# Moving the adding transfers of a weight row ahead of the sums of squares, and a store of zeros ahead of a load

## The chip, the cores and the metric

The kernel runs on one core of one Trainium2 chip. The metric is the device time of one execution in microseconds (us). The kernel before takes 734.59 us (median of three runs, 734.38 to 735.34).

## The reference, cut to what matters

Two blocks work on 4096 tokens (16 sequences of 256) of width 256. The first is a gated recurrence, the second a mixture of 16 experts, of which each token uses four.

```
x = x + layernorm(L0_attn(layernorm(x)))     # xp = x @ W_in.T, gates = xp @ W_gate.T + b_gate,
                                             # a scan over the sequence, then @ W_out.T
h = layernorm(x)
logits = h @ router_weight.T + router_bias   # top 4 of 16, softmax over the four
gate_up = einsum('th,ehd->etd', h, gate_up_proj) + gate_up_proj_bias
glu = min(gate, 7) * sigmoid(1.702 * min(gate, 7))
out = einsum('etd,edh->eth', (clip(up, -7, 7) + 1) * glu, down_proj) + down_proj_bias
x = x + layernorm(sum over experts of router_score * out)
```

A normalised row sums to zero over its 256 columns. The kernel uses that: it leaves the last column of the normalised row out, puts a one in its place, subtracts the last row of each expert's gate_up weights from all its other rows, and puts the bias where the last row was. The diff touches this subtraction.

## The kernel before, in words

**Stages.** The tokens go through the recurrence in eight blocks of 512, in a software pipeline of steps `step(s)`: block s gets its gates, block s-1 its scan and output product, block s-2 its second normalisation and its router logits, block s-3 its expert rows. Then come 143 tiles of 128 rows, each of one expert, and at the end the sums are normalised and stored. Each engine runs its own list of instructions in the order in which it is written, and waits on semaphores in front of an instruction; what stands behind a waiting instruction waits too. Within a step the lists go by gate chunk c = 0 to 7, and a place in them is written here as (s, c). Tables give the weight work its places: `SQUARE_AT` for `squares(n)`, `CONV_DN` and `CONV_GU` for `high(n)`.

**Weights.** W holds 24 parts of 1024 columns in float32: 8 of the down weights and 16 of the gate_up weights, one for each expert. `squares` on ScalarE (ACT) takes the sum of squares of a part, all 24 one after the other; from these comes the scale with which `high` and `low` (on VectorE, DVE) turn the parts into two float16 halves. The down parts are squared at (0, 6) to (1, 3). The gate_up parts c0, c1 and c2 have the place (1, 5), c3 (1, 6), c4 and c5 (1, 7), c6 (2, 0), c7 (2, 2), and c15, the last, (3, 6).

**The negative row.** SyncE (SP) loads the last rows (`nrow`), DVE turns their sign, SP stores them to `neg_mem`; then GpSimd (POOL) issues 16 adding transfers, one for each expert, of 512 KB each: the row from `neg_mem`, spread over 128 partitions, is added to the part in W by the DMA engines. In the kernel before such a transfer waits until both parts of its pair have been squared. SP writes the bias row into W's last partition when all 16 have landed (`bias_in`), and the first `high` of a gate_up part, at (4, 2), waits for that.

**SP's queue.** SP issues all plain transfers in the order of its list. `ring_x(b)` stores block b-5 of the residual (`store_x1`, when `r3_ready` says that it is normalised), waits for the store to land, and loads block b of x into the same buffer. Behind `ring_x(5)` stand two transfers of 4 MB each that fill the two DRAM buffers `sums` with zeros; the tile stage adds into these. `stats_x(5)` on DVE, at the start of step 3, needs block 5.

Of the kernel before, what the change touches and what calls it, by code (L numbers as in the profile page):

```python
# [19 lines left out]
P = 128  # L20
BATCH, SEQ, DIM = 16, 256, 256
TOKENS = BATCH * SEQ
# [6 lines left out]
NTILE = TOKENS // P  # L29
GATES = 4 * DIM  # L30
CHUNKS = GATES // P
E, TOPK, FF = 16, 4, 256
# [28 lines left out]
SUMS = 2  # L61
BATCHES = ((0, 1, 2, 3), (4, 5, 6), (7,))
PART = 1024
PARTS_GU, PARTS_DN = E * KT * 2 * FF // PART, E * KT * DIM // PART
PARTS = PARTS_GU + PARTS_DN
# [67 lines left out]
def build(nc, x, w_in, w_gate, b_gate, rms_w, w_out, w_router, b_router, w_gu, b_gu, w_dn, b_dn,  # L133
# [3 lines left out]
    ALU = mybir.AluOpType  # L137
# [5 lines left out]
    with ctx:  # L143
        def sb(name, shape, dt=f32):
            return ctx.enter_context(nc.sbuf_tensor(name, shape, dt))

        def sem(name):
            return ctx.enter_context(nc.semaphore(name))
# [6 lines left out]
        sums = [nc.dram_tensor(f"sums{a}", [TOKENS + (E + SPARE) * P, DIM], f32, kind="Internal").ap() for a in range(SUMS)]  # L155
# [15 lines left out]
        zero = sb("zero", [P, DIM])  # L171
# [117 lines left out]
        s_moe = [sem(f"s_moe{n}") for n in range(PARTS_GU // 2)]  # L289
        squared, peak_ready, peak_mm = sem("squared"), sem("peak_ready"), sem("peak_mm")  # L290
        scale_ready, high_done, low_done = sem("scale_ready"), sem("high_done"), sem("low_done")
        blk_in = [sem(f"blk_in{b}") for b in range(NBLK)]
        nrow_in, nrow_ready, nrow_out, minus_done = sem("nrow_in"), sem("nrow_ready"), sem("nrow_out"), sem("minus_done")
        bias_in, bias_out, brow_ready = sem("bias_in"), sem("bias_out"), sem("brow_ready")
        s_down, wr_ready = sem("s_down"), sem("wr_ready")
        hi_ready, lo_ready, one_ready = sem("hi_ready"), sem("lo_ready"), sem("one_ready")
# [26 lines left out]
        zero_ready, zero_sent, x1_sent = sem("zero_ready"), sem("zero_sent"), sem("x1_sent")  # L323
# [17 lines left out]
        def order(n):  # L341

            return PARTS_GU + n if n < PARTS_DN else n - PARTS_DN
# [4 lines left out]
        def held(table, top, eng, first, n):  # L348

            _, values = nc.values_load_multi_w_load_instructions(  # L350
                table[0:1, ds(first, n)], engines=[eng], min_val=0, max_val=top,
                skip_runtime_bounds_check_because="the table holds counts, capped at the last spare tile")
            return values
# [35 lines left out]
        def source(c):  # L389
            return W[:, (place(c) + 1) * PART:(place(c) + 2) * PART]  # L390
# [13 lines left out]
        def _(sp):  # L404
# [30 lines left out]
            sp.dma_start(bias_mem, brow).then_inc(bias_out, 16)  # L435
            sp.wait_ge(nrow_ready, 1)
            sp.dma_start(neg_mem, nrow).then_inc(nrow_out, 16)

            def store_x1(t):
                sp.wait_ge(r3_ready, t + 1)  # L440
                sp.dma_start(out_v[:, BT * t:BT * (t + 1), :], block_x(t)).then_inc(x1_sent, 16)

            def ring_x(b):
                store_x1(b - XRING)
                sp.wait_ge(x1_sent, 16 * (b - XRING + 1))
                sp.wait_ge(x2_ready, b - XRING + 1)
                load_x(b)

            ring_x(XRING)
            sp.wait_ge(zero_ready, 1)  # L450
            for a in range(SUMS):
                sp.dma_start(sums[a][0:TOKENS, :].rearrange("(n p) d -> p n d", p=P),
                             zero[:, :].unsqueeze(1).to_broadcast([P, NTILE, DIM])).then_inc(zero_sent, 16)
            ring_x(XRING + 1)
            sp.wait_ge(minus_done, 16 * E)
            sp.wait_ge(bias_out, 16)
            sp.dma_start(W[P - 1:P, (GU0 + 1) * PART:(GU0 + 1 + PARTS_GU) * PART]
                         .rearrange("o (e k x) -> o e k x", e=E, k=KT)[:, :, KT - 1, :],
# [323 lines left out]
        def _(act):  # L782
# [86 lines left out]
            def squares(n):  # L869
                c = order(n)  # L870
                if c == PARTS_GU:
                    act.wait_ge(s_down, 16 * PARTS_DN // 2)
                if c < PARTS_GU and c % 2 == 0:
                    act.wait_ge(s_moe[c // 2], 16)
                act.wait_ge(squared, n + 1)
                nc.scalar.activation(junk, source(c), ACT.Square, accum_out=ssq[:, c:c + 1]).then_inc(squared, 1)  # L876

# [13 lines left out]
            def weight_work(s, c):  # L891
                for n, at in enumerate(SQUARE_AT):
                    if at == (s, c):
                        squares(n)
                for n, at in enumerate(CONV_DN + CONV_GU):
                    if at == (s, c):
                        high(n)
# [130 lines left out]
        @block.gpsimd  # L1028
        def _(pool):
            def wait(s, n):  # L1030
                pool.wait_ge(s, n)
                if not isinstance(n, int):
                    pool.nop(nofuse=True)

            def scatter(t):

                b = t % 2
                per = BT * TOPK // 2
                pool.wait_ge(slot_ready, t + 1)
                pool.wait_ge(lo_ready, t + 1)  # L1040
                for jk in range(BT * TOPK if t < NBLK - 2 else AHEAD):
                    lane = jk % 2
                    if t or jk >= 2:
                        pool.wait_ge(rows_sent[lane], 16 * (per * t + jk // 2))
                    idx = slot[b][:, jk:jk + 1].bitcast(u32)
                    pool.indirect_dma_start(routed, bass.IndirectOffsetOnAxis(ap=idx, axis=0),  # L1046
                                            rows[b][:, jk // TOPK, :], None).then_inc(rows_sent[lane], 16)

            pool.wait_ge(nrow_out, 16)
            for e in range(E):  # L1050
                if e % 2 == 0:
                    pool.wait_ge(s_moe[e // 2], 16)
                    pool.wait_ge(squared, 2 + PARTS_DN + e + 1)
                pool.dma_start(W[:, (GU0 + 1 + e) * PART:(GU0 + 2 + e) * PART].rearrange("p (k x) -> p k x", k=KT),  # L1054
                               neg_mem[e:e + 1, :].unsqueeze(1).to_broadcast([P, KT, 2 * FF]),
                               accum_op=ALU.add).then_inc(minus_done, 16)

            for t in range(NBLK - 1):
                scatter(t)

            def late_row(n):
                t, jk = divmod(BT * TOPK * (NBLK - 2) + AHEAD + n, BT * TOPK)
                if jk == 0:
                    pool.wait_ge(slot_ready, t + 1)
                    pool.wait_ge(lo_ready, t + 1)
                idx = slot[t % 2][:, jk:jk + 1].bitcast(u32)
                pool.indirect_dma_start(routed, bass.IndirectOffsetOnAxis(ap=idx, axis=0),
                                        rows[t % 2][:, jk // TOPK, :], None).then_inc(rows_sent[jk % 2], 16)

            for j in range(TILES):  # L1070
                u = j % YU
                pool.wait_ge(meta_in[j % MU], 16 * (j // MU + 1))
                if j == 0:
                    pool.wait_ge(zero_sent, 16 * SUMS)
                pool.wait_ge(y2_ready, j + 3)
                if j >= SUMS:
                    pool.wait_ge(y_sent[(j - SUMS) % YU], 16 * ((j - SUMS) // YU + 1))
                pool.indirect_dma_start(sums[j % SUMS], bass.IndirectOffsetOnAxis(ap=dst[j % MU], axis=0),  # L1078
                                        yb[u], None, compute_op=ALU.add).then_inc(y_sent[u], 16)
                if j % 2 and j // 2 < 2 * BT * TOPK - AHEAD:  # L1080
                    late_row(j // 2)

            pool.wait_ge(x1_sent, 16 * (NBLK - 1))
            for g in range(NBLK - 1):
                pool.wait_ge(yz_ready, g + 1)
                pool.dma_start(out_v[:, BT * g:BT * (g + 1), :], z[g], accum_op=ALU.add).then_inc(out_sent, 16)
# [480 lines left out]
```

## Time and profile before

| what | value |
|---|---|
| median of three runs | 734.59 us |
| the profiled execution's own time | 735.17 us |
| its span | 733.4 us |
| TensorE (PE) busy | 626.0 us, 85% |
| DVE busy | 516.5 us, 70% |
| ACT busy | 459.2 us, 63% |
| POOL busy | 395.2 us, 54% |

Times in the trace are counted from the span's start. The steps of the recurrence take up its first 260 us or so. The page's share of DMA is the mean over the core's 16 DMA engines of the time that their packets took; as packets overlap, it can be somewhat over one. SPq is SP as it issues transfers; the duration of such a row is the time that the issue took.

### The profile page before, as it was taken

What the parts mean: (1) busy time and instruction counts of PE and PEld (TensorE: products, weight loads), DVE (VectorE), ACT (ScalarE), POOL (GpSimd) and SP (SyncE); (2) the same over time, 40 slices, a digit from 0 to 9 for tenths busy, and PEclk for the clock granted to TensorE, in tenths of its full rate; (3) what the DMA queues carried; (4) which work ended last, traced back from release to release, by engine and by line L of the source; (5) the groups of instructions that cost most, each with busy time, mean ns of one, the idle gap of its engine ahead of it and who ended that gap; (6) DMA issues with size and microseconds to landing.
All of it is one profiled execution on the core that took longest, in us unless ns stands there. A gap on an engine that the chain in (4) does not pass through costs nothing.

```text
span 733.4 us, 13293 instructions
## 1 busy us (share of the span) xinstructions
PE 626.0 (85%) x3690; PEld 400.4 (55%) x3690; DVE 516.5 (70%) x1472; ACT 459.2 (63%) x929; POOL 395.2 (54%) x298
## 2 busy tenths in 40 slices
PE   6988979797999848799989999999999999984640
PEld 2454636373655546466656666666666666653420
DVE  3726596968878897877877777777777777650794
ACT  3788887647575643576656776766767767661044
POOL 0004212346777676667788776666666656576022
PEclk9999999679989956999999999999999999996555
DMA  7979999773232335456678977777776766755998
GB/s 243 419 308 150 219 266 300 184 198 118 88 120 89 118 118 154 130 103 115 118 133 174 186 154 117 109 116 115 109 115 103 116 111 104 107 65 59 317 226 145
DMA packets 110695, 114.34 MB, mean 156 GB/s; under 512 B 31426, under 2 KB 100306, under 8 KB 108962
## 3 DMA queue, kind: packets, MB, share of 16 engines
q0 software_dynamic: 34784, 49.70, 40.0%
q1 hardware_dynamic: 75842, 63.79, 29.0%
q8 instruction: 35, 0.57, 0.3%
q14 instruction: 34, 0.28, 0.1%
HBM read 54.94 MB, written 58.51 MB: 155 GB/s over the span
## 4 chain that ended last, share of the span: by engine, by line
PE 63%; DVE 22%; ACT 5%; issue 4%; DMA 4%; POOL 1%; DVEq 0%; SPq 0%; ACTq 0%; POOLq 0%
PE PS L544 9%; PE PS L695 8%; PE PS L697 8%; PE PS L696 8%; PE PS L723 4%; PE PS L709 4%; PE PS L724 4%; PE PS L725 4%; PE PS L684 4%; PE PS L579 3%; DMA sums<-arena 3%; DVE small L1161 2%; PE PS L571 2%; PE PS L601 2%; DVE W L1321 1%
## 5 line engine op out<-in xcount | busy, mean ns | idle before, releaser
L1078 POOL DMA_INDIRECT sums<-arena x143 | 222.6, 1556 | 103.7 <-DMA sums<-arena 55.2
L1046 POOL DMA_INDIRECT routed<-arena,small x104 | 119.3, 1148 | 71.5 <-DMA routed<-arena,small 58.7
L1468 DVE TENSOR_SCALAR arena<-PS,small 128x256 f32<-128x256 f32 x143 | 77.7, 544 | 83.1 <-ACT arena L979 82.9
L544 PE MATMUL PS<-arena 128*128 128x512 f32 x256 | 130.8, 648 | 4.1 <-ACT arena L784 2.2
L979 ACT ACTIVATE arena<-PS,small 128x256 f32<-128x256 f32 x143 | 67.8, 474 | 100.2 <-PE PS L697 100.2
L784 ACT ACTIVATE arena<-PS 128x512 f16<-128x512 f16 (+1 forms) x179 | 103.9, 590 | 32.6 <-PE PS L589 11.0
L695 PE MATMUL PS<-W,arena 128*128 x286 | 109.3, 382 | 0.0
L696 PE MATMUL PS<-W,arena 128*128 x286 | 109.2, 382 | 0.0
L697 PE MATMUL PS<-W,arena 128*128 x286 | 108.9, 381 | 0.0
L723 PE MATMUL PS<-W,arena 128*128 x286 | 78.6, 275 | 6.9 <-DVE arena L1442 5.7
L724 PE MATMUL PS<-W,arena 128*128 x286 | 78.7, 275 | 0.0
L725 PE MATMUL PS<-W,arena 128*128 x286 | 78.6, 275 | 0.0
L1054 POOL DMA_DIRECT2D W<-neg_mem x16 | 19.7, 1471 | 107.5 <-ACT W L876 107.5
L544 PEld LDWEIGHTS PS<-arena 128*128 128x128 f32 x256 | 49.1, 205 | 51.9 <-issue 44.4
L784 ACT ACTIVATE arena<-PS,arena 128x256 f32<-128x256 f32 x143 | 69.0, 483 | 10.1 <-PE PS L725 9.9
L1470 DVE SCALAR_TENSOR_TENSOR arena<-arena,small 128x256 f32<-128x256 f32 x143 | 69.4, 486 | 5.1
L1442 DVE SCALAR_TENSOR_TENSOR arena<-PS,small,arena 128x256 f16<-128x256 f32 x143 | 68.4, 479 | 5.1 <-ACT arena L784 4.9
L784 ACT ACTIVATE arena<-PS,small 128x256 f16<-128x256 f32 x143 | 68.0, 476 | 2.0 <-PE PS L709 2.0
L684 PEld LDWEIGHTS PS<-ident,arena 128*128 128x128 f16 x572 | 43.0, 98 | 37.6 <-issue 8.3
L804 ACT ACTIVATE arena<-PS,small 128x512 f32<-128x512 f32 x64 | 43.7, 683 | 27.4 <-PE PS L544 23.7
L709 PE MATMUL PS<-K,arena 128*128 128x128 f32 x286 | 55.7, 276 | 3.6 <-DVE arena L1442 3.6
L1469 DVE SCALAR_TENSOR_TENSOR arena<-arena,PS 128x256 f32<-128x256 f32 x143 | 58.7, 411 | 0.0
(183 smaller groups left out, 1019.0 us busy)
## 6 DMA issues: line engine op xcount, KB each, us to landing
arena<-routed SPq DMA_DIRECT2D x143, 128.0 KB, 2.5
W<-w_gu SPq DMA_DIRECT2D x8, 1024.0 KB, 23.9
W<-neg_mem POOLq DMA_DIRECT2D x16, 512.0 KB, 9.5
sums<-zero SPq DMA_DIRECT2D x2, 4096.0 KB, 35.6
W<-sums SPq DMA_DIRECT2D x16, 512.0 KB, 8.8
X<-x SPq DMA_DIRECT2D x8, 512.0 KB, 6.2
W<-w_dn SPq DMA_DIRECT2D x4, 1024.0 KB, 11.4
out<-X SPq DMA_DIRECT2D x7, 512.0 KB, 3.2
```

Of the source, the lines that this page charges most:

```text
L544: last = mm(PS[:, 2 + c % 2, :], WcT[:, k, c * P:(c + 1) * P], xT[:, k, :], start=(k == 0), stop=(k == KT - 1))
L695: mm(acc, xq[j % NX][:, k, :], hi, start=(k == 0), stop=False)
L696: mm(acc, xq[j % NX][:, k, :], lo, start=False, stop=False)
L697: last = mm(acc, xq[j % NX][:, KT + k, :], hi, start=False, stop=(k == KT - 1))
L709: last = nc.tensor.transpose(PS[:, act_bank(j), k * P:(k + 1) * P], act_[j % NB][:, k * P:(k + 1) * P], ident)
L723: mm(acc, ah[j % 2][:, k, :], hi, start=(k == 0), stop=False)
L724: mm(acc, ah[j % 2][:, k, :], lo, start=False, stop=False)
L725: last = mm(acc, al[j % 2][:, k, :], hi, start=False, stop=(k == KT - 1))
L784: return nc.scalar.activation(o, i, ACT.Copy, **kw)
L1046: pool.indirect_dma_start(routed, bass.IndirectOffsetOnAxis(ap=idx, axis=0), rows[b][:, jk // TOPK, :], None).then_inc(rows_sent[lane], 16)
L1078: pool.indirect_dma_start(sums[j % SUMS], bass.IndirectOffsetOnAxis(ap=dst[j % MU], axis=0), yb[u], None, compute_op=ALU.add).then_inc(y_s ...
L1468: L.send(v.tensor_scalar(up[j % 2], acc[:, FF:2 * FF], gu_hi, gu_lo, ALU.min, ALU.max))
```

## The change

Three edits. (1) POOL's adding transfers no longer wait for the squares of their pair: they wait for the weights (`s_moe`) and, the first one, for `neg_mem`. They count on eight semaphores, one for each pair, in place of one. (2) `squares` of a gate_up part waits, at the first of each pair, for both adding transfers of the pair (`minus_done[c // 2]`), where it waited for the load of the weights. So it takes the squares of the weights after the subtraction. SP's store of the bias row waits for all pairs and for all squares. (3) The two transfers of zeros move on SP from behind `ring_x(5)` to right behind the store of `neg_mem`.

```
-            ring_x(XRING)
             sp.wait_ge(zero_ready, 1)
             for a in range(SUMS):
                 sp.dma_start(sums[a]..., zero...).then_inc(zero_sent, 16)
...
             ring_x(XRING)
             ring_x(XRING + 1)
-            sp.wait_ge(minus_done, 16 * E)
+            for n in range(PARTS_GU // 2):
+                sp.wait_ge(minus_done[n], 32)
+            sp.wait_ge(squared, 1 + PARTS)
...
                 if c < PARTS_GU and c % 2 == 0:
-                    act.wait_ge(s_moe[c // 2], 16)
+                    act.wait_ge(minus_done[c // 2], 32)
...
                 if e % 2 == 0:
                     pool.wait_ge(s_moe[e // 2], 16)
-                    pool.wait_ge(squared, 2 + PARTS_DN + e + 1)
                 pool.dma_start(W..., neg_mem[e:e + 1, :]..., accum_op=ALU.add)
-                               .then_inc(minus_done, 16)
+                               .then_inc(minus_done[e // 2], 16)
```

On ACT, the stretch of (1, 5) to (1, 7), first of the kernel before. `ACTIVATE W,small<-W` are the squares, the one that waits for `s_moe0` being c0; the rows of `arena<-PS,small` are gate chunks.

```order
L784 ACTIVATE arena<-arena 128x1024 [waits gate_act]
L876 ACTIVATE W,small<-W 128x1024 [waits squared,s_moe0]
L876 ACTIVATE W,small<-W 128x1024 [waits squared]
L876 ACTIVATE W,small<-W 128x1024 [waits squared,s_moe1]
L804 ACTIVATE arena<-PS,small 128x512 [waits gate_mm]
L876 ACTIVATE W,small<-W 128x1024 [waits squared]
L888 ACTIVATE W<-W,small 128x2x512 [waits scale_ready]
L784 ACTIVATE arena<-PS 128x512 [waits xT_mm,gate_mm]
```

And the same stretch of the kernel after.

```order
L787 ACTIVATE arena<-arena 128x1024 [waits gate_act]
L879 ACTIVATE W,small<-W 128x1024 [waits squared,minus_done0]
L879 ACTIVATE W,small<-W 128x1024 [waits squared]
L879 ACTIVATE W,small<-W 128x1024 [waits squared,minus_done1]
L807 ACTIVATE arena<-PS,small 128x512 [waits gate_mm]
L879 ACTIVATE W,small<-W 128x1024 [waits squared]
L891 ACTIVATE W<-W,small 128x2x512 [waits scale_ready]
L787 ACTIVATE arena<-PS 128x512 [waits xT_mm,gate_mm]
```

Nothing moved on ACT; c0 and c2 wait for another semaphore.

On SP, from the load of the gate_up weights on, first of the kernel before.

```order
L431 DMA W<-w_gu 128x2048 x8
L433 DMA Bdn<-b_dn 16x256
L435 DMA bias_mem<-arena 16x512 [waits brow_ready]
L437 DMA neg_mem<-arena 16x512 [waits nrow_ready]
L441 DMA out<-X 128x4x256 [waits r3_ready]
L408 DMA X<-x 128x4x256 [waits x2_ready,x1_sent]
L452 DMA sums<-zero 128x32x256 [waits zero_ready]
L452 DMA sums<-zero 128x32x256
```

And of the kernel after.

```order
L432 DMA W<-w_gu 128x2048 x8
L434 DMA Bdn<-b_dn 16x256
L436 DMA bias_mem<-arena 16x512 [waits brow_ready]
L438 DMA neg_mem<-arena 16x512 [waits nrow_ready]
L441 DMA sums<-zero 128x32x256 [waits zero_ready]
L441 DMA sums<-zero 128x32x256
L446 DMA out<-X 128x4x256 [waits r3_ready]
L409 DMA X<-x 128x4x256 [waits x2_ready,x1_sent]
```

The zeros moved ahead of the store of residual block 0 and the load of x block 5, on the same queue.

## Rows read from the trace of the kernel before

**Rows 1.** The page's chain that ended last, shares by engine.
```profile
PE 63%; DVE 22%; ACT 5%; issue 4%; DMA 4%; POOL 1%; DVEq 0%; SPq 0%; ACTq 0%; POOLq 0%
```
**Rows 2.** The page's groups: busy, mean ns; idle before and its releaser.
```profile
L1054 POOL DMA_DIRECT2D W<-neg_mem x16 | 19.7, 1471 | 107.5 <-ACT W L876 107.5
```
**Rows 3.** Timeline of ACT: start, us, what; in brackets idle before.
```profile
52.44 1.04 ACT L876 ACTIVATE W<-W 128x1024 bf16<-128x1024 f32 x1
...
54.85 1.06 ACT L876 ACTIVATE W<-W 128x1024 bf16<-128x1024 f32 x1
...
59.35 0.69 ACT L804 ACTIVATE arena<-PS,small 128x512 f32<-128x512 f32 x1 [3.35 <-PE PS L544]
...
63.59 1.07 ACT L876 ACTIVATE W<-W 128x1024 bf16<-128x1024 f32 x1
...
70.79 1.04 ACT L876 ACTIVATE W<-W 128x1024 bf16<-128x1024 f32 x1
...
140.96 1.15 ACT L888 ACTIVATE W<-W,small 128x1024 f16<-128x1024 f32 x1 [3.53 <-DMA W<-bias_mem]
```
**Rows 4.** Timeline of SP's queue.
```profile
30.50 0.42 SPq L437 DMA_DIRECT2D neg_mem<-arena  x1
76.62 0.40 SPq L441 DMA_DIRECT2D out<-X  x1
...
80.32 22.59 SPq L452 DMA_DIRECT2D sums<-zero  x2
107.86 8.66 SPq L441 DMA_DIRECT2D out<-X  x1
123.37 0.37 SPq L408 DMA_DIRECT2D X<-x  x1
```
**Rows 5.** DMA issues: KB each, us to landing.
```profile
neg_mem<-arena SPq DMA_DIRECT2D x1, 32.0 KB, 22.0
```
**Rows 6.** Stretches: length, busy (x count) of five engines, PE's clock, DMA share, GB/s.
```profile
50.00:52.00 2.00, 0.28 (x1) 0.00 (x0) 1.12 (x2) 1.97 (x3) 0.00 (x0) 1.00 0.16 60
...
56.00:58.00 2.00, 2.00 (x9) 1.52 (x9) 0.00 (x0) 0.00 (x0) 2.00 (x2) 0.97 0.25 40
...
60.00:65.00 5.00, 4.22 (x12) 1.76 (x11) 4.24 (x24) 4.97 (x10) 2.44 (x2) 1.00 1.04 172
...
95.00:105.00 10.00, 7.87 (x30) 3.90 (x28) 9.51 (x21) 9.24 (x18) 2.44 (x2) 1.00 1.11 231
110.00:120.00 10.00, 10.00 (x58) 7.54 (x57) 7.66 (x25) 6.69 (x11) 0.00 (x0) 0.96 1.09 386
```
**Rows 7.** Timeline of POOL, asked for in short stretches too.
```profile
55.38 2.61 POOL L1054 DMA_DIRECT2D W<-neg_mem  x2 [54.94 <-ACT W L876]
...
89.48 2.44 POOL L1054 DMA_DIRECT2D W<-neg_mem  x2 [10.45 <-ACT W L876]
...
90.21 1.71 POOL L1054 DMA_DIRECT2D W<-neg_mem  x1
...
96.87 1.71 POOL L1054 DMA_DIRECT2D W<-neg_mem  x1
```
**Rows 8.** DMA issues at 91.5, 98.3, 81.7, 107.9 and 147.0 us, each alone.
```profile
W<-neg_mem POOLq DMA_DIRECT2D x1, 512.0 KB, 13.1
...
W<-neg_mem POOLq DMA_DIRECT2D x1, 512.0 KB, 13.3
...
sums<-zero SPq DMA_DIRECT2D x1, 4096.0 KB, 40.4
...
out<-X SPq DMA_DIRECT2D x1, 512.0 KB, 15.5
...
X<-x SPq DMA_DIRECT2D x1, 512.0 KB, 4.3
```
**Rows 9.** Timeline of DVE: the statistics of x block 5.
```profile
103.57 1.40 DVE L1112 BATCH_NORM_STATS2 small<-X 128x6 f32<-128x256 f32 x4
```
**Rows 10.** One stretch of step 4, columns as in rows 6.
```profile
143.00:154.60 11.60, 11.51 (x32) 7.45 (x33) 6.88 (x19) 5.25 (x9) 4.10 (x5) 0.50 0.82 274
```

More of the change, by code:

```diff
@@ L292, in build @@
         blk_in = [sem(f"blk_in{b}") for b in range(NBLK)]
-        nrow_in, nrow_ready, nrow_out, minus_done = sem("nrow_in"), sem("nrow_ready"), sem("nrow_out"), sem("minus_done")
+        nrow_in, nrow_ready, nrow_out = sem("nrow_in"), sem("nrow_ready"), sem("nrow_out")
+        minus_done = [sem(f"minus_done{n}") for n in range(PARTS_GU // 2)]
         bias_in, bias_out, brow_ready = sem("bias_in"), sem("bias_out"), sem("brow_ready")
@@ L437, in _ @@
             sp.dma_start(neg_mem, nrow).then_inc(nrow_out, 16)
+            sp.wait_ge(zero_ready, 1)
+            for a in range(SUMS):
+                sp.dma_start(sums[a][0:TOKENS, :].rearrange("(n p) d -> p n d", p=P),
+                             zero[:, :].unsqueeze(1).to_broadcast([P, NTILE, DIM])).then_inc(zero_sent, 16)
             def store_x1(t):
@@ L449, in _ @@
             ring_x(XRING)
[L450 to L453, printed above, removed]
             ring_x(XRING + 1)
-            sp.wait_ge(minus_done, 16 * E)
+            for n in range(PARTS_GU // 2):
+                sp.wait_ge(minus_done[n], 32)
+            sp.wait_ge(squared, 1 + PARTS)
             sp.wait_ge(bias_out, 16)
@@ L873, in squares @@
                 if c < PARTS_GU and c % 2 == 0:
-                    act.wait_ge(s_moe[c // 2], 16)
+                    act.wait_ge(minus_done[c // 2], 32)
                 act.wait_ge(squared, n + 1)
@@ L1052, in _ @@
                     pool.wait_ge(s_moe[e // 2], 16)
-                    pool.wait_ge(squared, 2 + PARTS_DN + e + 1)
                 pool.dma_start(W[:, (GU0 + 1 + e) * PART:(GU0 + 2 + e) * PART].rearrange("p (k x) -> p k x", k=KT),
                                neg_mem[e:e + 1, :].unsqueeze(1).to_broadcast([P, KT, 2 * FF]),
-                               accum_op=ALU.add).then_inc(minus_done, 16)
+                               accum_op=ALU.add).then_inc(minus_done[e // 2], 16)
             for t in range(NBLK - 1):
```

## The prediction

> **What bounds the kernel now.** I read the chain of waits first, by shares: PE and DVE carry most of it, DMA 4% [rows 1]. In the list of that chain the steps of the recurrence pass from PE to DVE to ACT and back all the time, so an engine that stops there for longer than its own slack stops the others, and no later place in the steps gives the time back. Next, the costliest groups: POOL spends 107.5 us in front of the adding transfers, waiting for ACT's squares [rows 2]. Nothing on the chain waits for POOL there, so this wait is free, and its removal is worth nothing by itself. Then the timelines of ACT, SP and POOL around the places of the diff, and the DMA shares of stretches. ACT starts c0 at 52.44 and c2 at 54.85, then idles 3.35 us until PE has its next gate chunk at 59.35 [rows 3]. That idle time is all the slack that ACT has: c4 at 63.59 and c6 at 70.79 lie in a stretch in which ACT is busy nearly without a break (4.97 of 5 us [rows 6]).
>
> The DMA engines are full between 60 and 65 us with one pair or two of adding transfers under way: share 1.04 at only 172 GB/s [rows 6]. The same engines move 386 GB/s while they write mostly zeros (110 to 120 us), and 231 GB/s when zeros and adding transfers run together (95 to 105 us). An adding transfer is thus a slow one, and it is the DMA engines that it fills, not POOL.
>
> **Edit 1 and 2: the squares now wait for the adding transfers.** The first adding transfer waits for `neg_mem`. Its store is issued at 30.50 [rows 4] and lands 22.0 us later [rows 5], behind the weights in the same queue: 52.5. So POOL can issue the first pair at about 52.6 rather than at 55.38 [rows 7], and then all 16 without a stop.
>
> How fast do they land? Before, the pair issued at 89.48 ran beside the zeros; its second transfer was issued at 90.21 [rows 7] and landed 13.1 us later [rows 8], at 103.3, which is 13.8 after the pair's start. The next pair was issued while this one was still under way; its second transfer started at 96.87 [rows 7] and landed 13.3 later [rows 8], at 110.2. From pair to pair 6.9 us, with zeros beside them. After the change zeros run beside them too (edit 3). So the first pair lands at 52.6 + 13.8 = 66.4, and the others follow each 6.9 later: 73.3, 80.2, 87.1, 94.0 and so on, the eighth at 66.4 + 7 x 6.9 = 114.7.
>
> Against this the places of the squares, shifted by what has been lost so far. c0 would start at 52.44 and waits until 66.4; c1 follows; c2 waits for the second pair, 73.3. From c2's start at 54.85 to the end of its two instructions ACT takes about 1.15 us, so the gate chunk that began at 59.35 begins at about 74.5: 15.2 us late. c4 then comes at 63.59 + 15.2 = 78.8 and waits until 80.2: 1.4 more, 16.6 in all. c6 comes at 70.79 + 16.6 = 87.4, the fourth pair is there at 87.1. All later squares come after their pairs. Term one: +16.6 us. Behind the waiting square on ACT stand the gate chunks and the copies of the transposed x of step 2; PE runs out of work a few us after 62 and waits with it, DVE too.
>
> Bounds: if the adding transfers had the DMA engines to themselves, a pair of 1.05 MB would take 6.1 us (at 172 GB/s), the first one landing near 62 and c2 near 68: about +11. If the zeros went through wholly first, +28 (below). I take the value between, since it is the measured one for both together.
>
> A lower price stands in the notes. The Trainium skill (page "DMA: Bandwidth & Descriptors", section "Anatomy of one DMA — SWDGE (gpsimd) path") fits a transfer issued from GpSimd as about 2.0 us plus its bytes over 436e3; by that, as an estimate, a pair alone would take 4.4 us and ACT would lose next to nothing. The trace speaks against it for adding transfers: 172 GB/s at a full share.
>
> **Edit 3: zeros ahead of the load of x block 5.** The weights leave the DMA engines idle from about 50.3 on (share 0.16 in 50 to 52 [rows 6]); the zeros stand right behind them in SP's queue and start there. The adding transfers' data start about 2.1 us after the issue (55.38 [rows 7], and the share of 0.25 in 56 to 58 [rows 6] puts the start near 57.5), so at 54.7. Until then the zeros move 4.4 us x 386 GB/s = 1.70 MB. Beside the adding transfers, which take 1.05 MB in 6.9 us = 152 GB/s, they get 231 - 152 = 79 GB/s: 60 us x 79 = 4.74 MB by 114.7. Of 8.39 MB 1.95 are left, 5.1 us at 386: the zeros land at about 119.8.
>
> The store of residual block 0 is ready at 76.62 [rows 4] + 16.6 = 93.2, but stands behind the zeros. Before, the next store stood behind them in the same way: issued at 107.86 [rows 4], landing 15.5 later [rows 8] at 123.4, when the zeros had landed at 81.6 + 40.4 = 122.0; so 1.4 behind them. After: 121.2. Then the load of block 5 goes out at once, as at 123.37 [rows 4], and takes 4.3 us when nothing else runs [rows 8]: 125.5. DVE wants it at 103.57 [rows 9] + 16.6 = 120.2, and behind that wait on DVE stand the norms for which PE, and through it ACT, wait. Term two: +5.3 us. The least is 0, if the zeros get a larger share early; the most is about 12, if the adding transfers take all and ACT is only 11 late. The two terms trade against each other: what the zeros lose the adding transfers gain, and the sum of both moves much less than either.
>
> **What goes.** The bias row no longer comes behind the last adding transfer: it follows the last square, which lies far ahead of (4, 2). ACT's wait of 3.53 us at 140.96 [rows 3] goes. I count it as nothing, since DVE is busy through it without a wait, and PE and ACT's next copy wait for DVE. POOL's scatters can begin sooner after their rows, and DMA has room after 120; nothing on the chain waited for either. What may count is the clock: from 134.7 to 154.6 PE has 0.50 (1.2 GHz), though it is busy for 11.51 of the 11.6 us from 143.0 on [rows 10]. At full clock that work takes half: 5.8 us. The low clock began before ACT's wait, so I don't book its end as a gain; on the other hand two new stops of PE may each cost some at 1.2 GHz behind them. Net 0, between -6 and +6.
>
> **The sum.** Profiled execution 735.17 + 16.6 + 5.3 = 757.1. The median of the runs lies 0.6 below the profiled one: 756.5 us.
>
> **Rivals.**
> *Zeros first.* The DMA engines serve the queue that is already running, and the adding transfers only start at 50.3 + 8.39 MB / 386 = 72.0. The pairs then land at about 80, 86, 92: c2 ends at 87, 28 us behind, c4 about 0.5 more; x block 5 is then in time. 735.2 + 28.2 - 0.6 = 763. For it: the zeros have no gap between descriptors. Against it: 231 GB/s with both, of which most was adding transfers.
> *Adding transfers first.* ACT loses 11, the zeros end at 120 all the same, DVE waits about 12 for block 5: 735.2 + 23 - 0.6 = 758. The same time within the range, with the wait in another place.
> *No wait for block 5.* The zeros are through before 114, and only term one is paid: 751. For it: the zeros got part of the time in 95 to 105; against it: only 79 GB/s.
> *Not slower.* Queued 16 deep rather than two, the adding transfers go at the 386 GB/s of plain ones and keep four fifths of it beside the zeros: four of them, 2.10 MB, need 6.8 us from 54.7 on, c2 starts at 61.5 and ends at 62.7, ACT is 3.3 late. With the bias row early the low clock of step 4 goes too: -5.8. 735.2 - 2.5 - 0.6 = 732. It decides from the point where the second pair lands before 64, where ACT's loss is below 5.8. The skill's fit named above points the same way. Against it: two transfers already filled the engines (1.04).
>
> **Chances.** Forecast 0.55 (its own range 750 to 763), zeros first 0.15, adding transfers first 0.12, no wait for block 5 0.10, not slower 0.05, rest 0.03. The range 745 to 769 covers the four slower cases with the clock's bounds. Less than 0.2% is about what a measurement of this kernel can't tell from no change. Faster 0.05, same 0.03, slower 0.92.
>
> **What would show it.** Right: ACT's squares at (1, 5) released by the landing of adding transfers, with about 14 and 4 us idle, POOL issuing all 16 in a row from 52.6, PE idle from about 62 to 76; DVE waiting for x block 5 near 120; no wait for the bias row. Wrong: the pairs less than 5 us apart; block 5 landed before DVE asks; a stretch of the steps after 160 us that is shorter than before by more than the clock explains.

## The result, and the profile after

The kernel after takes 752.57 us (median of four runs, 751.0 to 754.59), the kernel before in the same comparison 734.49 us (727.98 to 735.34): slower, ratio 1.0286, 95% interval 1.0231 to 1.0342. The forecast was 756.5 with a range of 745 to 769. A ratio, here and below, compares the fast runs of both kernels, while a median takes all of them (in the experiments also one of the kernel before at 3481.38 us and one of e2 at 854.72), so a ratio is not the quotient of the medians. The profiled execution has a span of 750.0 us, 16.6 more than before.

The page's chain that ended last has gained DMA and SP's queue, shares by engine; before they had 4% and 0% [rows 1].

```profile
PE 53%; DVE 19%; DMA 15%; SPq 4%; issue 4%; ACT 4%; POOL 1%; DVEq 0%; ACTq 0%; POOLq 0%
```

DMA stands at 15% and SP's issues at 4%; by line, the store `out<-X`, the adding transfers `W<-neg_mem` and the store `neg_mem<-arena` have 3% each. The timeline of ACT shows the waits for the adding transfers (start, us, engine, line, what; in brackets the idle time before and what ended it). L879 are the squares, L807 the gate chunks.

```profile
68.14 1.06 ACT L879 ACTIVATE W<-W 128x1024 bf16<-128x1024 f32 x1 [15.56 <-DMA W<-neg_mem]
...
75.00 1.06 ACT L879 ACTIVATE W<-W 128x1024 bf16<-128x1024 f32 x1 [4.53 <-DMA W<-neg_mem]
...
76.05 0.67 ACT L807 ACTIVATE arena<-PS,small 128x512 f32<-128x512 f32 x1
...
81.91 1.06 ACT L879 ACTIVATE W<-W 128x1024 bf16<-128x1024 f32 x1 [1.57 <-DMA W<-neg_mem]
...
85.19 0.67 ACT L807 ACTIVATE arena<-PS,small 128x512 f32<-128x512 f32 x1
...
88.82 1.06 ACT L879 ACTIVATE W<-W 128x1024 bf16<-128x1024 f32 x1 [0.19 <-DMA W<-neg_mem]
...
158.57 1.15 ACT L891 ACTIVATE W<-W,small 128x1024 f16<-128x1024 f32 x1 [1.61 <-DVE W L1323]
```

c0, c2, c4 and c6 each wait for a DMA: 15.56 + 4.53 + 1.57 + 0.19 = 21.8 us. The gate chunk that followed at 59.35 [rows 3] now starts at 76.05. The first conversion of a gate_up part no longer waits for the bias row (it waited 3.53 us at 140.96 [rows 3]) but 1.61 us for DVE.

POOL's timeline: all 16 adding transfers go out in one piece.

```profile
53.08 19.94 POOL L1056 DMA_DIRECT2D W<-neg_mem  x16 [52.62 <-DMA neg_mem<-arena]
```

SP's queue: the zeros, the store of residual block 0 (its issue takes 17.26 us), and the load of x block 5 as soon as the store has landed.

```profile
31.14 32.58 SPq L441 DMA_DIRECT2D sums<-zero  x2
94.50 17.26 SPq L446 DMA_DIRECT2D out<-X  x1
119.73 0.37 SPq L409 DMA_DIRECT2D X<-x  x1
```

DVE waits for that block, which it did not before [rows 9].

```profile
123.38 1.41 DVE L1114 BATCH_NORM_STATS2 small<-X 128x6 f32<-128x256 f32 x4 [1.91 <-DMA X<-x]
```

The stretches (length, busy and count of PE, PEld, DVE, ACT and POOL, PE's clock, DMA share, GB/s): full DMA engines at low throughput, an idle PE, and the clock that falls behind it.

```profile
64.00:67.00 3.00, 0.00 (x0) 0.00 (x0) 0.00 (x0) 0.00 (x0) 3.00 (x8) 0.77 1.12 234
67.00:70.00 3.00, 0.00 (x0) 0.00 (x0) 0.00 (x0) 1.83 (x3) 3.00 (x5) 0.50 1.11 232
...
85.00:112.00 27.00, 23.23 (x116) 15.27 (x117) 15.94 (x54) 24.46 (x43) 0.00 (x0) 1.00 1.11 233
163.00:174.60 11.60, 11.60 (x32) 7.27 (x31) 6.94 (x15) 5.16 (x9) 2.06 (x3) 0.50 0.75 251
```

The first two rows are the stop: nothing computes but, from 68.14 on, ACT's squares, and POOL is still issuing. PE stands for 19.05 us, from 60.4 to 79.4:

```profile
79.42 5.30 PE L547 MATMUL PS<-arena 128*128 128x512 f32 x8 [19.05 <-ACT arena L787]
```

Step by step the shift can be read from one small transposition that PE does once in each of the steps 1 to 8; the rows are those of steps 2, 3 and 8. First the kernel before, from the timeline of PE:

```profile
76.45 0.33 PE L560 MATMUL PS<-K,small 128*16 128x128 f32 x1 [0.38 <-DVE small L1104]
107.69 0.39 PE L560 MATMUL PS<-K,small 128*16 128x128 f32 x1 [3.91 <-DVE small L1104]
...
270.28 0.38 PE L560 MATMUL PS<-K,small 128*16 128x128 f32 x1 [1.48 <-DVE small L1104]
```

The same rows after:

```profile
94.33 0.28 PE L563 MATMUL PS<-K,small 128*16 128x128 f32 x1 [1.75 <-DVE small L1106]
127.50 0.39 PE L563 MATMUL PS<-K,small 128*16 128x128 f32 x1 [4.70 <-DVE small L1106]
...
289.89 0.38 PE L563 MATMUL PS<-K,small 128*16 128x128 f32 x1 [1.48 <-DVE small L1106]
```

17.9 late in step 2, 19.8 in step 3, 19.6 in step 8: all the loss is made by two stops, and the steps behind them neither add to it nor give any back. From there to the end of the span 3.0 us are regained (19.6 against 16.6).

### The profile page after: what moved, and what is told of

The parts are those of the page before. It is cut to its first block, busy times and chain, and to the rows that moved or that the text cites. A ratio compares the mean times of both kernels' runs of the same rounds, so it can differ in the third digit from the quotient of the medians.

```text
span 750.0 us, 13290 instructions
## 1 busy us (share of the span) xinstructions
PE 625.8 (83%) x3690; PEld 400.4 (53%) x3690; DVE 516.2 (69%) x1472; ACT 459.3 (61%) x929; POOL 393.1 (52%) x298
## 3 DMA queue, kind: packets, MB, share of 16 engines
q1 hardware_dynamic: 75842, 63.79, 28.6%
## 4 chain that ended last, share of the span: by engine, by line
PE 53%; DVE 19%; DMA 15%; SPq 4%; issue 4%; ACT 4%; POOL 1%; DVEq 0%; ACTq 0%; POOLq 0%
PE PS L698 8%; PE PS L700 8%; PE PS L699 8%; PE PS L547 4%; PE PS L726 4%; PE PS L727 4%; PE PS L712 4%; PE PS L728 4%; PE PS L687 4%; DMA out<-X 3%; DMA W<-neg_mem 3%; DMA neg_mem<-arena 3%; DMA sums<-arena 2%; DMA routed<-arena,small 2%; PE PS L582 2%
## 5 line engine op out<-in xcount | busy, mean ns | idle before, releaser
L547 PE MATMUL PS<-arena 128*128 128x512 f32 x256 | 132.4, 655 | 22.0 <-ACT arena L787 20.7
L787 ACT ACTIVATE arena<-PS,small 128x256 f16<-128x256 f32 x143 | 68.1, 476 | 2.0 <-PE PS L712 2.0
L807 ACT ACTIVATE arena<-PS,small 128x512 f32<-128x512 f32 x64 | 43.7, 683 | 23.9 <-PE PS L547 20.5
L687 PE MATMUL PS<-ident,arena 128*128 128x128 f16 x572 | 55.2, 219 | 3.4 <-ACT arena L787 3.1
```

Of the source, the lines that this page charges most:

```text
L547: last = mm(PS[:, 2 + c % 2, :], WcT[:, k, c * P:(c + 1) * P], xT[:, k, :], start=(k == 0), stop=(k == KT - 1))
L687: last = nc.tensor.transpose(xT16[:, k * P:(k + 1) * P], xrow[j % UN][:, k * P:(k + 1) * P], ident16[:, :])
L787: return nc.scalar.activation(o, i, ACT.Copy, **kw)
```

## The experiments

Six kernels, each compared with runs of the kernel before on the same chip. Those runs had medians of 733.49 (first four kernels) and 734.61 (last two) and lay mostly between 725 and 740, more widely than the three runs that were shown at first; differences of 2 or 3 us are not settled by the times. A trace is of one execution, so the traces are compared by the places in the steps, where a wait can be named, and not by their spans. Of the six, e4 is slower by more than 2%; e1, e2 and e7 are slower than the kernel before, but their intervals don't say whether by more or less than 2%; e3 and e6 are the same within 2%.

**e1_zeros_back: edits 1 and 2 without edit 3.**

```
+            ring_x(XRING)
             sp.wait_ge(zero_ready, 1)
             for a in range(SUMS): ...           # the two transfers of zeros
-            ring_x(XRING)
             ring_x(XRING + 1)
```

> The kernel after with the two transfers of zeros put back behind ring_x(5); the squares still wait for the adding transfers. My theory (the adding transfers' own DMA time, stretched by the zeros beside them, is what ACT waits for): without zeros the pairs land 9.4 us after the first issue at 53.1 and then each 6.0 later (62.5, 68.5, 74.4), the gate chunk of (1, 6) begins near 69.7, 10.4 late instead of 16.7, c4 waits another 0.4, and x block 5 is there long before DVE asks: +11 against the kernel before, 745 to 746 us. Rival (the zeros don't slow the adding transfers; what they cost is only the wait for x block 5, 1.9 us): pairs at 68, 75, 82 as in the kernel after, 750 to 751.

Measured: 745.45 us, ratio 1.0217 (1.0143 to 1.0291). ACT's timeline:

```profile
62.09 1.06 ACT L879 ACTIVATE W<-W 128x1024 bf16<-128x1024 f32 x1 [9.45 <-DMA W<-neg_mem]
...
67.21 1.06 ACT L879 ACTIVATE W<-W 128x1024 bf16<-128x1024 f32 x1 [2.80 <-DMA W<-neg_mem]
...
68.27 0.67 ACT L807 ACTIVATE arena<-PS,small 128x512 f32<-128x512 f32 x1
```

The gate chunk begins 8.9 us late instead of 16.7; no wait for x block 5 is left, and the time is the one that the theory gave. So the zeros nearly double what ACT waits. The pairs land 5.1 apart, faster than the 6.0 I had taken. A stretch of the same kernel shows the rate: with many adding transfers queued the engines do 206 GB/s at a share of 1.13, against 172 with one or two pairs [rows 6].

```profile
75.00:85.00 10.00, 8.09 (x31) 4.09 (x30) 7.21 (x23) 10.00 (x18) 0.00 (x0) 0.95 1.13 206
```

**e2_zeros_early_only: edit 3 without edits 1 and 2.** The kernel before, with one edit:

```
             sp.dma_start(neg_mem, nrow).then_inc(nrow_out, 16)
+            sp.wait_ge(zero_ready, 1)
+            for a in range(SUMS): ...           # the two transfers of zeros
...
             ring_x(XRING)
-            sp.wait_ge(zero_ready, 1)
-            for a in range(SUMS): ...
             ring_x(XRING + 1)
```

> The kernel before with edit 3 alone: the zeros right behind the store of neg_mem, adding transfers still behind the squares. My theory: nobody waits for an adding transfer until the bias row, so a slower landing beside the zeros costs nothing; the zeros end near 95 because four or five pairs share the engines with them, x block 5 lands at 102 to 106 against DVE's question at 103.6: 0 to +3 us against the kernel before, 734 to 738. Rival (early zeros cost something in any case, by contention with scatters, loads or the weights): +5 or more.

Measured: 743.54 us, ratio 1.0163 (1.0053 to 1.0273). The expectation missed, and the time is in the range that was given for the rival. The mechanism named is there, but bigger: DVE waits 4.55 us for x block 5.

```profile
110.25 1.41 DVE L1113 BATCH_NORM_STATS2 small<-X 128x6 f32<-128x256 f32 x4 [4.55 <-DMA X<-x]
```

The store ahead of that load landed late, as SP's queue shows:

```profile
76.78 14.18 SPq L446 DMA_DIRECT2D out<-X  x1
103.33 0.37 SPq L408 DMA_DIRECT2D X<-x  x1
```

Its load then went beside adding transfers and took 6.9 us. The zeros ended at 96.6, about where I had let them end (95), but I had let the fifth and sixth pair, issued at 91.5 and 98.2, take nothing from the store; its landing at 103.3 says that they did. So far the rival's contention is part of it.

DVE reaches that wait 2.1 us late already. The four gate products behind the transposition of step 2 took twice as long as in the kernel before, first the row of before:

```profile
76.62 1.88 PE L544 MATMUL PS<-arena 128*128 128x512 f32 x4
```

and in e2 the row and its stretch, at a clock of 0.50:

```profile
76.79 3.62 PE L545 MATMUL PS<-arena 128*128 128x512 f32 x4
...
76.80:80.40 3.60, 3.60 (x6) 1.06 (x5) 0.00 (x0) 3.15 (x7) 2.40 (x2) 0.50 1.10 232
```

No run shows that edit 3 brought this on. Edit 3 alone makes the kernel slower; the wait for x block 5 is the part of it that is shown.

**e3_late_squares_zeros_back: early adding transfers, and squares that come when they have landed.**

```
-  (1, 5), (1, 5), (1, 5), (1, 6), (1, 7), (1, 7), (2, 0), (2, 2), (2, 5), (2, 5), (2, 6), (2, 7), (3, 0), (3, 5), (3, 5), (3, 6)
+  (2, 0), (2, 2), (2, 4), (2, 5), (2, 5), (2, 6), (2, 7), (3, 0), (3, 2), (3, 4), (3, 4), (3, 5), (3, 5), (3, 6), (3, 7), (3, 7)
```

and the zeros as in e1.

> The kernel after with the zeros put back behind ring_x(5), and the sixteen squares of the gate_up parts at later places: c0 at (2, 0), then (2, 2), (2, 4), (2, 5) twice, (2, 6), (2, 7), (3, 0), (3, 2), (3, 4) twice, (3, 5) twice, (3, 6), (3, 7) twice; so each pair has landed when its squares come. My theory (the stop of ACT at (1, 5) is the cost, not the early adding transfers): no square waits for a DMA, and what is left is the six squares (1.25 us each) that moved from step 1, where DVE bounds the end of the step, into steps 2 and 3, some of them in gaps of ACT: +1 to +4 us against the kernel before, 735 to 739. Rival (the adding transfers in a row cost by something else than ACT's wait, for instance contention with the loads of x): +8 or more with no square waiting.

Measured: 735.64 us against 733.49, ratio 1.0044 (0.9993 to 1.0095). No square of a gate_up part waits for a DMA: the gate chunk of (1, 6) begins at 59.47 (59.35 before), and the row of c0 at (2, 0) has no wait in front of it.

```profile
59.47 0.69 ACT L807 ACTIVATE arena<-PS,small 128x512 f32<-128x512 f32 x1 [6.81 <-PE PS L547]
...
71.29 1.04 ACT L879 ACTIVATE W<-W 128x1024 bf16<-128x1024 f32 x1
```

With edit 1 and the semaphores of edit 2 in place, what edits 1 and 2 had cost in e1 is gone but for some 2 us that the interval doesn't tell from nothing. It is the waiting ACT that cost, not the early transfers.

**e4_late_squares: the same squares, zeros early.**

> The kernel after, zeros early, with the squares at the same later places as in the kernel e3. My theory: ACT waits for no adding transfer, but the zeros still hold the queue until about 118, so x block 5 still lands near 123 while DVE asks for it near 105: the wait of 1.9 us becomes about 18, and the time stays within 3 us of the kernel after, 750 to 755. Rival (the wait for x block 5 isn't set by the zeros but comes after the store of residual block 0, which shifts with the steps): the store goes out at 77, the load follows, and the kernel takes 735 to 740.

Measured: 754.88 us, ratio 1.0326 (1.0256 to 1.0396). No square of a gate_up part waits for a DMA (c0 is the first row below), and yet the kernel is as slow as the kernel after. At step 3 all of the lateness comes from DVE's wait (second row): the transposition (third row) is 19.5 late, where the kernel after was 19.8 late.

```profile
69.23 1.04 ACT L879 ACTIVATE W<-W 128x1024 bf16<-128x1024 f32 x1
...
123.08 1.41 DVE L1114 BATCH_NORM_STATS2 small<-X 128x6 f32<-128x256 f32 x4 [19.52 <-DMA X<-x]
...
127.19 0.38 PE L563 MATMUL PS<-K,small 128*16 128x128 f32 x1 [21.83 <-DVE small L1106]
```

The SP queue of this kernel shows the store waiting in line, not the steps being late:

```profile
75.08 36.53 SPq L446 DMA_DIRECT2D out<-X  x1
119.39 0.37 SPq L409 DMA_DIRECT2D X<-x  x1
```

Ready at 75.08, landed at 119.4, within 0.4 us of the kernel after, where it was ready only at 94.50. So that moment goes with the DMA work ahead and beside it, 8.4 MB of zeros and 8.4 MB of adding transfers from 50 us on, and not with ACT. Behind step 3 this kernel loses another 8.4 us by step 8 and gets 6.5 back by the end of its span; that its total agrees so well with that of the kernel after is in part chance.

**e6_neg_first: the row is stored before the weights are loaded.** e1, with the store of `neg_mem` moved ahead of the load of the gate_up weights.

```
+            sp.wait_ge(nrow_ready, 1)
+            sp.dma_start(neg_mem, nrow).then_inc(nrow_out, 16)
             for c in range(0, PARTS_GU, 2):
                 sp.dma_start(W..., w_gu...).then_inc(s_moe[c // 2], 16)
...
-            sp.wait_ge(nrow_ready, 1)
-            sp.dma_start(neg_mem, nrow).then_inc(nrow_out, 16)
```

> The kernel e1 (zeros behind ring_x(5), squares behind the adding transfers) with the store of neg_mem moved on SP ahead of the load of the gate_up weights, so that POOL can issue a pair as soon as its weights land (from about 35 us) and not at 53. Theory (ACT waits for the adding transfers' own DMA work): the engines are then shared between the loads and the adding transfers, the loads end near 58 rather than 50, the first pair lands near 53, the second near 62; c2 ends near 63, ACT is about 4 late instead of 9 to 11: +4 against the kernel before, 737 to 740. Rival (the loads, being far ahead in the other queue, get nearly all until they end, and the adding transfers start at 50 anyway): first pair near 60, second near 66, +8, 741 to 744.

Measured: 736.67 us against 734.61, ratio 1.0041 (1.0004 to 1.0078), just below the range of the theory. POOL's first issues, then ACT's timeline:

```profile
34.90 7.56 POOL L1056 DMA_DIRECT2D W<-neg_mem  x6 [34.45 <-DMA W<-w_gu]
...
55.59 1.06 ACT L879 ACTIVATE W<-W 128x1024 bf16<-128x1024 f32 x1 [2.76 <-DMA W<-neg_mem]
...
62.72 1.06 ACT L879 ACTIVATE W<-W 128x1024 bf16<-128x1024 f32 x1 [4.79 <-DMA W<-neg_mem]
...
63.77 0.67 ACT L807 ACTIVATE arena<-PS,small 128x512 f32<-128x512 f32 x1
```

POOL issues the first pair at 34.9, and the gate chunk is 4.4 us late instead of 8.9. So half of ACT's lateness at (1, 6) without zeros came from the row's store standing behind the weights. That the other half is the adding transfers' own DMA time is argued, not shown: the loads of the weights share the engines with them here until the last pair is issued at 58.7.

**e7_plain_copies: no add.** The kernel after with `accum_op` left out.

```
-                               neg_mem[e:e + 1, :]..., accum_op=ALU.add).then_inc(minus_done[e // 2], 16)
+                               neg_mem[e:e + 1, :]...).then_inc(minus_done[e // 2], 16)
```

> The kernel after with the sixteen transfers as plain ones, without the add: the same 512 KB each, issued by POOL at the same places, write the row over the weights instead of adding it (the subtraction is left out, and with it the right weights). Theory (it is the add that makes them slow: 172 GB/s alone against 386 for plain transfers): beside the zeros a pair takes about 4.1 us instead of 6.9, the first lands near 61 and the second near 65, ACT is about 6 or 7 late instead of 17; the zeros end near 94, before the store of residual block 0, so that x block 5 is in time: +6 to +7, 739 to 742. Rival (what counts is the issue and the start on POOL or the 2 KB pieces, not the add): landings at 68, 75, 82 as in the kernel after, 750 to 754.

Measured: 744.58 us, ratio 1.0151 (1.0087 to 1.0215). ACT's timeline:

```profile
64.29 1.06 ACT L879 ACTIVATE W<-W 128x1024 bf16<-128x1024 f32 x1 [11.69 <-DMA W<-neg_mem]
...
67.62 1.06 ACT L879 ACTIVATE W<-W 128x1024 bf16<-128x1024 f32 x1 [1.00 <-DMA W<-neg_mem]
...
68.67 0.67 ACT L807 ACTIVATE arena<-PS,small 128x512 f32<-128x512 f32 x1
```

And a stretch of it:

```profile
65.00:70.00 5.00, 0.00 (x0) 0.00 (x0) 0.00 (x0) 3.97 (x8) 0.00 (x0) 0.53 1.04 411
```

Beside the zeros pairs land 3.3 us apart instead of 6.9, the engines move 411 GB/s instead of 232, and nobody waits for x block 5. So without the add a pair takes half the DMA time. The packets differ with it. Packets, MB and share of the two queues (q0 is POOL's, q1 SP's), first in the kernel after from 75 to 95 us, then in e7 from 64 to 82:

```profile
q0 software_dynamic: 1581, 3.04, 82.0%
q1 hardware_dynamic: 1574, 1.61, 29.1%
...
q0 software_dynamic: 1591, 5.79, 78.6%
q1 hardware_dynamic: 1597, 1.62, 25.3%
```

Both queues send the same number of packets in either kernel, and POOL's carry about 1.9 KB with the add and 3.6 KB without, while the zeros' carry 1.0 KB. Whether it is the adding or the smaller packets that cost the time, e7 does not separate. But the first pair lands 11.4 us after its issue at 52.9, where I expected 8: ACT is still 9.3 late, and the total of 745 was missed by 3. Even at the price of plain transfers the change is slower. What makes up the 11.4 us (the issue on POOL, the zeros that are already queued, the landing) I did not take apart.

## Why the prediction was right

**Start and rate of the adding transfers.** Forecast: first issue at 52.6, pairs at 66.4, 73.3, 80.2, 87.1. Measured by the squares that they released: 53.08, then 68.1, 75.0, 81.9, 88.8. The step of 6.9 us, read from two pairs that ran beside zeros, held to a tenth; the first pair took 15.1 from its issue, not 13.8. The share held as well: 233 GB/s where I had 231, and by the rows under e7 152 of it for the adding transfers and 80 for the zeros, where I had 152 and 79. The other signs came too: idle times of 15.56 and 4.53 us in front of c0 and c2, all 16 issues in a row, no wait for the bias row; only PE's stop, 60.4 to 79.4, was longer than the 62 to 76 that I gave.

**Term one, forecast 16.6, measured 17.9.** The gate chunk of (2, 0), at 85.19 after, stood before at 67.30, as the timeline of ACT of the kernel before has it:

```profile
67.30 0.69 ACT L804 ACTIVATE arena<-PS,small 128x512 f32<-128x512 f32 x1
```

The 1.3 us between them come from the pairs, which landed 1.7 later than forecast. e1 and e3 show the two halves of the claim: take the zeros from beside the transfers and ACT loses 8.9 at (1, 6); move the squares behind the landings and it loses 0.1 there.

**Term two, forecast 5.3, measured 1.9.** The right mechanism, mis-sized. The store of residual block 0 landed at 119.7, not 121.2; the load took 3.6 us, not 4.3; and DVE asked at 121.5, as it came 1.3 later by term one. Each is a us or so, and the wait is a small difference of large numbers. The zeros landed at 118.3 (the second transfer issued at 31.6, 86.7 us to landing), where I had 119.8.

I had said that the two terms trade against each other, as what the zeros lose the adding transfers gain. e4 shows a trade of another kind: with no wait for the transfers left, the wait for the block grows from 1.9 to 19.5 us, as the block comes when it came before (DVE starts at 123.08, in the kernel after at 123.38). Both waits hang on the same transfers, and removing ACT's alone gains nothing; e3, which removes both, is as fast as the kernel before within what the runs can tell.

How the costs of the edits add up is less clear. By the ratios edits 1 and 2 alone cost 2.2%, edit 3 alone 1.6%, both together 2.9%, and the intervals reach from 0.6 to 1.1 points to either side: they don't tell 2.9 from the sum. In the traces the transposition of step 8, at 270.28 before, is 11.7 us late in e1 and 7.4 in e2 (the two rows below), 19.6 in the kernel after, which is close to the sum; but e2's has 2.1 us of low clock in it, and e1 was 8.4 late at step 3.

```profile
281.96 0.38 PE L563 MATMUL PS<-K,small 128*16 128x128 f32 x1 [1.48 <-DVE small L1106]
...
277.67 0.38 PE L561 MATMUL PS<-K,small 128*16 128x128 f32 x1 [1.48 <-DVE small L1105]
```

**The sum.** 17.9 + 1.9 = 19.8 at step 3, against 21.9 forecast. 16.6 are left at the end of the span. Of the 3.0 in between, 1.6 were regained up to ACT's last tile (18.0 late), for reasons left open. Another 1.1 came behind the last tile: there POOL's adding scatters into `sums` go one after another, and SP's first load of the sums follows ACT's last tile by 27.9 us before and 26.8 after. In the eight traces this distance lies between 21.7 (e4) and 28.6 (e6), and not in the order of the lateness. The total was closer than the terms: one was 1.3 short, the other 3.4 long, and 3.0 more were regained that I had not forecast. That 756.5 lies within 4 us of 752.57 owes something to luck; the places where ACT and DVE stop, and the 6.9 us between pairs, do not.

**What goes.** The wait for the bias row went, and was worth next to nothing, as booked (19.8 us late in step 3, 19.6 in step 8). The low clock of step 4 did not go: 0.50 from 163.0 to 174.6, with PE busy all the time, as from 143.0 to 154.6 before [rows 10]. So it was not the bias row's wait that brought it on, and the rival that counted on its end had no ground. Behind the stop at 64 PE's clock fell too, but it ran at full clock from 85 on, and in between it cost nothing that shows: from c4 to the next gate chunk ACT took 3.28 us, before 3.71.

**The rivals.** *Zeros first* is out: the pairs run at 6.9 beside zeros. *Adding transfers first* is out by the same rows. *No wait for block 5* came closest of them: the wait was 1.9, and by the total alone its 751 is nearer to 752.57 than the forecast. Only DVE's row tells the two apart. *Not slower* asked for adding transfers at the speed of plain ones: they are half as fast, and e7 shows that even plain ones lose time. The first pair of the kernel before, issued at 55.38 with the engines idle, landed 9.5 us later, by the issue and the landing of its second transfer:

```profile
56.24 1.76 POOL L1054 DMA_DIRECT2D W<-neg_mem  x1
...
W<-neg_mem POOLq DMA_DIRECT2D x1, 512.0 KB, 8.6
```

The price of the Trainium skill (page "DMA: Bandwidth & Descriptors", section "Anatomy of one DMA — SWDGE (gpsimd) path"), 4.4 us for a pair as an estimate, does not hold for such a pair with the add; no run here has a plain pair alone.

One sentence of mine was too sure: that 0.2% is about what a measurement can tell from no change. The runs of the kernel before, without the one at 3481.38, differ among themselves by up to 1.8% in one comparison.

## What to carry to other kernels

A wait that costs nothing (POOL's for the squares) is no reason to turn the order round: ask who waits after the turn, and whether it has other work in its list. DMA time is one budget: if transfers are moved early, count all bytes that must go through before the first one that somebody needs, at the rate of a stretch in which both kinds ran, and look for small urgent transfers (a store and a load of one block) that fall behind them in the same queue. Where two waits hang on the same transfers, removing the earlier one can only lengthen the later (e4, against e3).

## What the runs showed of the hardware

An adding transfer into SBUF costs about twice the DMA time of a plain one of the same size: 206 GB/s with many queued (e1) and 172 with one or two pairs under way (before), against 386 for the zeros alone (before) and 411 for plain copies beside zeros (e7). Its packets were also smaller, 1.9 KB against 3.6 KB for the plain copy, and which of the two counts is open.

Where POOL's queue and SP's queue both had work, they sent packets one for one: 1581 and 1574 in 20 us of the kernel after, 1591 and 1597 in 18 us of e7. So the bytes went by the size of the packets: about two thirds of them to the adding transfers (152 of 232 GB/s beside zeros in 1 KB packets), over three quarters to the plain copies (5.79 of 7.41 MB).

The first of a row of pairs came 15.1 us after its issue beside the zeros, 11.4 as plain copies beside the zeros, 9.2 without zeros (52.9 to 62.1 in e1): 1.8 to 3.4 times the later distance between pairs.
